# A decoder layer over 16 batches: approximate scores in four row groups, two bfloat16 transposes as DMAs

## What is computed

```python
# part 1: per head of 16 features: unit-length Fourier transforms of two projections,
#         one summed along the tokens, multiplied, transformed back, projected
q  = (x @ W_q.T).reshape(B, S, H, hd);  kv = (x @ W_kv.T).reshape(B, S, H, hd)
qf  = _l2_normalize_complex(fft(q));    kvf = cumsum(_l2_normalize_complex(fft(kv)), axis=1)
x = _layernorm(x + ifft(qf * kvf).real.reshape(B, S, D) @ W_o.T)
# part 2: causal attention of x on ctx, 16 heads of 16 features, keys = values = ctx
scores = jnp.einsum('bhqd,bhkd->bhqk', qh, kh) / math.sqrt(hd)
attn = softmax(where(causal, scores, MASKED_BIAS))
x = _layernorm(x + einsum('bhqk,bhkd->bhqd', attn, vh))
# part 3: x made ternary (threshold 0.33, +-0.5), times a ternary weight plus an offset
x_q = ternary_quantize(x, TH_X, SC_X)
x = _layernorm(x + jnp.einsum('bsd,od->bso', x_q, w_rram))
```

## Time and profile before

| | |
|---|---|
| median of 3 runs | 166.7 us (166.58 to 167.3) |
| the profiled execution | 166.76 us, its span 165.0 us |
| TensorE, VectorE, ScalarE, GpSimd busy | 146.9, 140.1, 128.2, 95.1 us |
| the chain that ended last | TensorE 47%, VectorE 28%, ScalarE 15%, issue 4%, GpSimd 4% |
| DMA | 14.56 MB, 29.5% of the 16 engines' span for the loads and stores |

### The profile page before, as it was taken

One profiled execution on the slowest core, in us unless ns is written; L12 is line 12 of the kernel. 1 busy time (PEld: TensorE's weight loads), 2 busy tenths in 40 slices (PEclk: granted clock), 3 DMA queues, 4 the chain that ended last, 5 costly groups with the idle time before them and its releaser, 6 DMA issues.

```text
span 165.0 us, 4546 instructions
## 1 busy us (share of the span) xinstructions
PE 146.9 (89%) x1612; PEld 98.6 (60%) x1629; DVE 140.1 (85%) x428; ACT 128.2 (78%) x342; POOL 95.1 (58%) x205
## 2 busy tenths in 40 slices
PE   7999999998999998999999999999899979897460
PEld 2746656567657556676776767765667647564230
DVE  0289899999999899989898989999899998868830
ACT  3466488888695986778989788878989979798642
POOL 4031550482690786156769834888477786778511
PEclk9999999999999999999999999999999999999855
DMA  3986566212033722122101554130312210101101
GB/s 107 288 270 177 175 161 216 79 52 68 0 116 106 204 63 60 35 57 76 36 0 38 162 156 99 56 105 2 90 41 43 96 28 2 36 32 36 64 34 64
DMA packets 16583, 14.56 MB, mean 88 GB/s; under 512 B 2352, under 2 KB 14512, under 8 KB 16560
## 3 DMA queue, kind: packets, MB, share of 16 engines
q1 hardware_dynamic: 16560, 14.26, 29.5%
HBM read 12.16 MB, written 2.10 MB: 86 GB/s over the span
## 4 chain that ended last, share of the span: by engine, by line
PE 47%; DVE 28%; ACT 15%; issue 4%; POOL 4%; POOLq 0%; ACTq 0%
PE p L727 8%; PE p L778 6%; PE p L747 6%; DVE x L2121 5%; ACT dev L1474 5%; PE p L762 5%; PE p L805 4%; PE p L768 3%; PE p L792 3%; ACT probs L1456 3%; PE p L785 3%; DVE ssq L2038 3%; PE p L733 2%; DVE unit L2054 2%; DVE r L2082 2%
## 5 line engine op out<-in xcount | busy, mean ns | idle before, releaser
L349 POOL TENSOR_SCALAR_AFFINE_SELECT probs<-probs 128x512 f32<-128x512 f32 x64 | 41.5, 664 | 10.1 <-ACT probs L1456 9.5
L2121 DVE TENSOR_REDUCE x<-p 128x4 f32<-128x512 f32 x64 | 41.7, 683 | 1.7 <-PE p L762 1.0
L1456 ACT ACTIVATE probs<-p 128x512 f32<-128x512 f32 x64 | 34.7, 595 | 4.7 <-PE p L778 4.5
L727 PE MATMUL p<-w_in,xT_s 128*128 128x512 f32 x64 | 30.3, 603 | 0.7 <-ACT w_in L1416 0.4
L343 POOL TENSOR_TENSOR rstd<-ve,power 128x1 f32<-128x1 f32 x48 | 26.9, 563 | 2.4
L338 POOL TENSOR_SCALAR ve<-spread 128x1 f32<-128x1 f32 x48 | 10.5, 218 | 29.6 <-ACT dev L1474 27.8
L1474 ACT ACTIVATE dev<-r,neg 128x256 f32<-128x256 f32 x48 | 24.2, 505 | 4.3 <-DVE neg L2094 4.2
L778 PE MATMUL p<-x1T,keys 32*128 32x128 f32 x512 | 18.8, 283 | 1.2 <-ACT x1T L1452 0.8
L778 PEld LDWEIGHTS p<-x1T,keys 32*128 32x128 f32 x512 | 15.8, 186 | 5.7 <-DVE x L2121 3.8
L785 PE MATMUL p<-probs,vals 128*32 128x128 f32 x512 | 18.1, 276 | 0.9 <-DVE att L2131 0.5
L762 PE MATMUL p<-keys,x1T_b 128*128 128x512 bf16 x47 | 16.4, 391 | 1.7 <-ACT probs L1456 1.1
(11 more groups left out here) (71 smaller groups left out, 282.8 us busy)
## 6 DMA issues: line engine op xcount, KB each, us to landing
vals<-ctxV SPq DMA_DIRECT2D x16, 256.0 KB, 2.9
x_s<-x SPq DMA_DIRECT2D x16, 128.0 KB, 2.7
xT_s<-xT SPq DMA_DIRECT2D x16, 128.0 KB, 2.6
keys<-ctxK SPq DMA_DIRECT2D x64, 32.0 KB, 2.2
out<-res SPq DMA_DIRECT2D x16, 128.0 KB, 1.7
wq_s<-w_q SPq DMA_DIRECT2D x1, 256.0 KB, 2.7
wkv_s<-w_kv SPq DMA_DIRECT2D x1, 256.0 KB, 3.7
woT_s<-w_oT SPq DMA_DIRECT2D x1, 256.0 KB, 3.9
```

Of the source, the lines that this page charges most:

```text
L349: nc.gpsimd.affine_select(out=part, in_=part, compare_op=ALU.is_ge, fill=0.0, base=0, pattern=[[0, GH], [1, TOK]], channel_multiplier=-1). ...
L727: last = nc.tensor.matmul(p[PROJ[n]][:], xT_s[n % XR][:, g, :], w_in[:, g, :], start=(g == 0), stop=(g == 1))
L1456: nc.scalar.activation(probs[n % 2][:, c, :, :].rearrange("p g q -> p (g q)"), p[ROWS + c][:], ACT.Exp, scale=HD ** -0.5).then_inc(exps[c], 1)
L2121: nc.vector.tensor_reduce(x1[n % X1R][:, GH * c:GH * (c + 1), HD], p[ROWS + c][:].rearrange("p (h k) -> p h k", h=GH), AX.X, ALU.max, nega ...
```

## The change

Five things change.

1. **Approximate scores.** `approximate(n)` is now one call with sixteen products: each takes one head's 32 rows and 128 columns, as `score` does. The head at slot s goes to the bank `APPROX[n][s]`. The key tile is compact, [128, 4, 128] instead of [128, 16, 128], and is loaded whole, constants included, with one DMA (256 KB instead of four times 32 KB). `blank`, `barred_s` and their waits are gone; the constants now encode nine queries to a slot. `row_max(n, c)` waits for one count after all sixteen.
2. **Banks.** The approximate and exact scores and the weighted values have banks by batch from all eight (`APPROX`, `SCORES`, `OUT`).
3. **Transposes.** `transpose_x1_b` and `transpose_xq` are DMAs from SBUF to SBUF in SP's queue, into `x1T_b` and `xqT_s`. TensorE's transposes and ScalarE's copies of both are gone.
4. **Start.** The folded input weights are copied half by VectorE, half by ScalarE. The first transposed inputs and the weights are loaded in another order. Rings of keys and values have six tiles, not five.
5. **Order.** All five lists are written in a new order.

```diff
-KV = 5
+KV = 6
...
+OUT = (0, 6, 0, 0, 5, 1, 1, 5, 2, 0, 2, 7, 1, 4, 2, 3)
+APPROX = ((0, 1, 7, 5), (2, 1, 4, 7), (6, 3, 5, 0), (1, 4, 3, 2), (5, 2, 0, 3), (1, 5, 6, 0),
...
-                for s in range(GH):
-                    sp.dma_start(keys[n % KV][SLOT * s:SLOT * s + HD, s::GH, :], ctxK[n, s]).then_inc(keys_in[n % KV], 16)
+                sp.dma_start(keys[n % KV][:], ctxK[n]).then_inc(keys_in[n % KV], 16)
...
+            def transpose_x1_b(n):
+                sp.dma_start_transpose(x1T_b[n % 2][:], x1_b[n % 2][:].rearrange("p h s -> p (h s)")).then_inc(x1T_b_in[n % 2], 16)
+
+            def transpose_xq(n):
+                sp.dma_start_transpose(xqT_s[n % 2][:], xq[n % 2][:]).then_inc(xqT_in[n % 2], 16)
...
-            def transpose_x1_b(n):
-
+            def approximate(n):
+
+                high = keys[n % KV][:].rearrange("p g k -> p (g k)").bitcast(bf16)[:, 1::2]
                 for g in range(GROUPS):
-                    last = nc.tensor.transpose(tile16(X1BT[n], GROUPS, TOK)[:, g, :],
-                                               x1_b[n % 2][:, GH * g:GH * (g + 1), :].rearrange("p h s -> p (h s)"),
-                                               ident_b[:])
-                last.then_inc(x1T_b_done, 1)
-
-            def approximate(n, c):
-
-                high = keys[n % KV][:, GH * c:GH * (c + 1), :].rearrange("p h k -> p (h k)").bitcast(bf16)
-                nc.tensor.matmul(p[ROWS + c][:], x1T_b[n % 2][:, c, :], high[:, 1::2],
-                                 start=True, stop=True).then_inc(approx[c], 1)
+                    for s in range(GH):
+                        slot = slice(SLOT * s, SLOT * (s + 1))
+                        last = nc.tensor.matmul(p[APPROX[n][s]][:, g * TOK:(g + 1) * TOK], x1T_b[n % 2][slot, g, :],
+                                                high[slot, g * TOK:(g + 1) * TOK], start=True, stop=True)
...
-            def transpose_xq(n):
-
-                for g in range(2):
-                    last = nc.tensor.transpose(tile16(XQT[n], 2, TOK)[:, g, :], xq[n % 2][:, g * 128:(g + 1) * 128], ident_b[:])
-                last.then_inc(xqT, 1)
 
...
-                        last = nc.tensor.matmul(p[ROWS + s][:, g * TOK:(g + 1) * TOK], keys[n % KV][slot, GH * g + s, :],
+                        last = nc.tensor.matmul(p[SCORES[n][s]][:, g * TOK:(g + 1) * TOK], keys[n % KV][slot, g, :],
...
-            def copy_x1T_b(n):
-
-                nc.scalar.activation(x1T_b[n % 2][:], tile16(X1BT[n], GROUPS, TOK), ACT.Copy).then_inc(x1T_b_copied, 1)
-
...
-            def copy_xqT(n):
-
-                nc.scalar.activation(xqT_s[n % 2][:], tile16(XQT[n], 2, TOK), ACT.Copy).then_inc(xqT_copied, 1)
...
-            def blank(buf):
-
-                nc.vector.tensor_copy(keys[buf][:], barred_s[:].unsqueeze(1).to_broadcast([128, HEADS, TOK])
-                                      ).then_inc(keys_blank[buf], 1)
+            def copy_w_in(g):
+
+                nc.vector.tensor_copy(w_in[:, g, :], p[g][:]).then_inc(w_in_ready[g], 1)
 
...
             def row_max(n, c):
 
-                nc.vector.tensor_reduce(x1[n % X1R][:, GH * c:GH * (c + 1), HD],
-                                        p[ROWS + c][:].rearrange("p (h k) -> p h k", h=GH), AX.X, ALU.max,
+                nc.vector.tensor_reduce(x1[n % X1R][:, c::GH, HD],
+                                        p[APPROX[n][c]][:].rearrange("p (h k) -> p h k", h=GH), AX.X, ALU.max,
                                         negate=True).then_inc(maxed[c], 1)
 
...
-    pairs = np.zeros((TOK, GH * SPARE), np.float32)
-    pairs[q, q // 3] = np.array([STEP_UP, 1.0, 1.0 / STEP_UP])[q % 3]
-    i, k = 3 * np.arange(GH * SPARE)[:, None], np.arange(TOK)[None, :]
-    bars = np.where(k > i + 2, -BARRED * STEP_UP,
-                    np.where(k == i + 2, -BARRED, np.where(k == i + 1, -LEAK, 0.0)))
-    barred = np.zeros((GH, SLOT, TOK), np.float32)
-    barred[:, HD, :] = 1.0
-    barred[:, HD + 1:, :] = bars.reshape(GH, SPARE, TOK)
-    trios = np.zeros((TOK, GH, SLOT - HD), np.float32)
-    trios[:, :, 1:] = pairs.reshape(TOK, GH, SPARE)
-    return trios, barred.reshape(GH * SLOT, TOK)
+    assert SHARE * SPARE >= TOK
+    pairs = np.zeros((TOK, SLOT - HD), np.float32)
+    pairs[q, 1 + q // SHARE] = 2.0 ** (TOP - STEP * (q % SHARE))
+    past = q[None, :] - SHARE * np.arange(SPARE)[:, None]
+    bars = np.where(past > 0, -2.0 ** (LEAK - TOP + STEP * np.clip(past, 0, SHARE)), 0.0)
+    return pairs, bars.astype(np.float32)
```

More of the change, by code:

```diff
@@ L149, in decoder_layer @@
         shift_done = [sem(f"shift_done{i}") for i in range(3)]
-        approx = [sem(f"approx{i}") for i in range(4)]
         maxed = [sem(f"maxed{i}") for i in range(4)]
@@ L215, in _ @@
-            sp.wait_ge(proj, 3)
-            load_xT(8)
+            load_x(4)
+            sp.wait_ge(x1_b_done, 1)
+            transpose_x1_b(0)
+            load_vals(1)
+            load_x(5)
+            load_x(6)
+            sp.wait_ge(x1_b_done, 2)
+            transpose_x1_b(1)
+            sp.wait_ge(x1_b_done, 3)
+            transpose_x1_b(2)
+            load_x(7)
+            load_keys(3)
+            load_x(8)
+            load_x(9)
+            load_keys(4)
+            load_keys(5)
@@ L809, in _ @@
             pe.wait_ge(warm_ready, 1)
-            busy(ROWS, 7)
+            busy(4, 7)
             pe.wait_ge(in_fold, 32)
@@ L976, in _ @@
+            pe.wait_ge(x1T_b_in[1], 48)
+            pe.wait_ge(keys_in[5], 16)
+            approximate(5)
+            pe.wait_ge(y_done, 9)
+            pe.wait_ge(x1T_copied, 4)
+            transpose_y(8)
+            pe.wait_ge(maxed[3], 5)
+            transpose_x1(4)
+            attend(7)
+            pe.wait_ge(maxed[3], 6)
             pe.wait_ge(masked[0], 3)
@@ new lines, in _ @@
+            cumulate(12)
+            pe.wait_ge(exps[2], 6)
+            pe.wait_ge(y_done, 12)
+            transpose_y(11)
+            pe.wait_ge(exps[3], 6)
+            pe.wait_ge(added[0], 11)
+            pe.wait_ge(x1T_b_in[1], 64)
+            pe.wait_ge(keys_in[1], 32)
+            approximate(7)
+            pe.wait_ge(added[2], 2)
+            transpose_x1(6)
+            pe.wait_ge(yT_copied, 12)
+            pe.wait_ge(xT_in[2], 48)
+            project(14)
+            pe.wait_ge(crossed, 13)
@@ new lines, in _ @@
+            pe.wait_ge(xT_in[3], 48)
+            project(15)
+            pe.wait_ge(maxed[0], 8)
+            pe.wait_ge(x1T_b_in[0], 80)
+            pe.wait_ge(keys_in[2], 32)
+            approximate(8)
+            pe.wait_ge(x1T_copied, 7)
+            pe.wait_ge(xqT_in[0], 32)
+            feed_forward(2)
+            pe.wait_ge(normed, 14)
+            attend(11)
+            pe.wait_ge(maxed[1], 9)
+            pe.wait_ge(y_done, 13)
+            transpose_y(12)
+            pe.wait_ge(added[2], 3)
@@ L1132, in _ @@
+            approximate(9)
+            pe.wait_ge(normed, 16)
+            pe.wait_ge(yT_copied, 14)
+            score(7)
+            pe.wait_ge(maxed[0], 10)
+            pe.wait_ge(masked[0], 7)
+            pe.wait_ge(vals_in[0], 32)
             weigh(6, 0)
+            weigh(6, 2)
+            pe.wait_ge(masked[3], 7)
             weigh(6, 3)
@@ L1274, in _ @@
+            pe.wait_ge(exps[1], 12)
+            pe.wait_ge(x1T_b_in[1], 112)
+            pe.wait_ge(keys_in[1], 48)
+            approximate(13)
+            pe.wait_ge(exps[2], 12)
+            pe.wait_ge(xqT_in[0], 64)
+            feed_forward(6)
+            weigh(10, 1)
+            weigh(10, 3)
+            pe.wait_ge(masked[2], 11)
+            weigh(10, 2)
+            pe.wait_ge(xqT_in[1], 64)
+            pe.wait_ge(exps[3], 12)
             feed_forward(7)
+            pe.wait_ge(maxed[3], 14)
@@ L2884 @@
     vals[..., HD] = 1.0
+    slots = np.zeros((BATCH, GH, SLOT, GROUPS, TOK), np.float32)
+    slots[:, :, :HD] = ctx.reshape(BATCH, TOK, GROUPS, GH, HD).transpose(0, 3, 4, 2, 1)
+    slots[:, :, HD] = 1.0
+    slots[:, :, HD + 1:] = bars[:, None, :]
     arrays = {
```

3044 lines of the change are left out of this document (1434 added, 1610 removed).

## The result

The changed kernel took 163.7 us (median of 4 executions, 162.0 to 164.9) against 166.7 before; the ratio is 0.973, 95% interval 0.968 to 0.979. The forecast was 162.1, with 156.5 to 169.0 around it. Six more executions of the same kernel in a later set gave 165.7 (163.9 to 166.3) beside 167.1, 0.990 [0.985, 0.994]; the median of all ten is 164.75. So the change is faster, by 1 to 2.7%, and the kernel with transposed DMAs scatters over 2.7% from execution to execution where the kernel before stays within 0.8% in every set. Since the ratios leave out what lies over 1.5% above a kernel's fastest, which here is ordinary scatter, I go by medians of all executions and give them beside the ratios.

What follows compares the result with a forecast made beforehand. VectorE and TensorE were taken to share the bound in the middle. Start 9.6, middle 128.0 and last stretch 22.7 gave a span of 160.3 us, time 162.1 with the 1.76 around it; range 156.5 to 169.

Steps and rivals of the forecast that it cites:

- Start: Time to VectorE's first sum of squares: 9.6 us instead of 10.13, with the two weight copies side by side.
- Middle: From VectorE's first sum of squares to its last row maximum: 121.0 us of VectorE work plus 7.0 idle, 128.0.
- that rival: TensorE, less busy, may be granted half clock speed in stretches: 168 us, chance 0.03.
- Last stretch: After VectorE's last row maximum: 21.3 us plus 1.4 for the last xq's uncovered landing, 22.7.
- The products: TensorE's sixteen approximate products of a batch: 0.55 us taken, at 35 ns each like the float32 exact scores.
- The landing: Transposed DMA in SP's queue, issue to landing: 2.9 us, as for 256 KB loads; outer ends 1.7 and twice 2.9.
- The rival of slow transposes: TensorE waits in order for transposed tiles, VectorE for its product; at 5.5 us a transpose, 172.7 us; chance 0.17.
- the two that I had called short: xq of batches 10 and 11: cover for the transposed landing about 0.8 us short each.
- my narrow ones: x1 of batches 0, 1 and 5: about 4 us of VectorE work as cover against 4.0 needed.
- my sign for wrong: SP's issue of a transpose over 1 us; another was TensorE waiting microseconds for DMA into x1T_b or xqT_s.
- Grouping: Rival: one count and four banks free at once delay row maxima 0.3 us a batch; 167.1 us, chance 0.13.
- it was not the bound: ScalarE falls from 128 to about 108 us without its copies; not the bound, it gives only earlier releases.

## Why the prediction was right, and which of its steps were not

The time was right in sign and within 1.6 us of the first set (2.7 of all ten), and part of that is luck: two errors of opposite sign. The profiled span, 163.2 us, is 2.9 above the forecast one: + 0.5 at the start, - 2.0 in the middle, + 4.4 at the end. The terms:

**Start, 9.6 forecast, 10.08 measured.** The two copies ran side by side only in part: VectorE's from 6.28, ScalarE's from 6.72, since the product it copies was ready only at 6.69. They ended at 7.32 instead of 7.37.

**Middle, 128.0 forecast, 126.0 measured.** The work was to be 121.0 and was 117.9; idle was to be 7.0 and was 8.1. The 12 instructions that moved behind the last row maximum account for 3.9 us (15.87 - 11.93) where I had 3.3. Most of the rest is overlap. Adding up the durations of the instructions that count as busy gives 166.5 us before and 163.9 after, while the busy time fell from 140.1 to 134.7: 26.4 us lay under a neighbour before, 29.2 after (2.1 of the 2.8 in the middle). My sum had no room for that. Why they overlap more was not tested; the order is the only thing that changed for most of them. Of the idle, 5.0 us came behind transposed tiles: 2.6 for approximate products and 2.4 for one feed-forward; what TensorE owed otherwise (y, r and rden, 2.0 us in the earlier trace rows) fell to 1.3. The last row maximum ended at 136.1 against 137.6, but VectorE was 93.5% busy up to it, not over 95%, and TensorE's busy time was 134.6 us, not 125 to 130. That sign did not follow from my own terms: 146.9 - 12.8 is 134.1. The clock was full up to there; that rival did not come in the middle.

**Last stretch, 22.7 forecast, 27.1 measured.** This is the step that failed, the mis-sized term. I took 3.3 us of work out of the middle and added none at the end, as if the end had been empty. Even with xq on TensorE the stretch is 23.65 us, 2.35 more than before's 21.3. With both transposes on TensorE it is 25.20, 3.9 more, while the middle is 129.33, 4.2 less: nearly all that left the middle there came back at the end. And I counted one uncovered landing (1.4 us). The order makes it two, one behind the other, and undoing xq's DMAs took 3.45 us off. VectorE's list, just ahead of the piece of it that I read, has the addition of 13 in front of xq 14; I read what stood between xq 15 and its own addition.

The clock has a part in the 3.45. In the first profile it was granted at half from 148.7 us on, before at half from 155.2, with xq on TensorE from 153.6; in the 3 us before it fell TensorE was busy for 1.31, 1.37 and 1.23 us. A feed-forward takes 1.46 us at half and 0.83 at full clock; three ran at half in the changed kernel, one with xq on TensorE, which is 1.3 us. In the second profile two did, and its last stretch was 26.69 us: 3.04 more than with xq on TensorE, 0.6 of it the clock's. So at least 2.2 to 2.4 us are the landings'.

**The products.** From start to start 0.34 us for sixteen, against 0.55 taken:

```profile
69.03 0.41 PE L827 MATMUL p<-keys,x1T_b 32*128 32x128 bf16 x16
69.37 0.70 PE L803 MATMUL p<-unit,upto_s 128*128 128x256 f32 x2
```

The 35 ns of the float32 passes was too dear; the Trainium skill's 3.07x (TensorE: Matmul & The Clock Gate), by which I had 0.30, was nearer. As forecast, the sum did not hang on it: 5.4 us more cost 0 to 2.

**The landing.** 2.9 us taken, medians 3.0 and 2.8 measured. The rule of the Trainium skill (VectorE: DVE Perf Modes, The three transpose paths) of 1309 ns a block, 5.2 us for four by my estimate, does not hold for these: four blocks land in 2.4 us and two in 2.3 when nothing is in the way, so blocks do not follow one another. The rival of slow transposes is wrong as stated, but its mechanism, TensorE waiting in order, came with single landings of 4 to 6 us and with the end. TensorE's 12.5 us of waits for xq are 6.1 for batches 13 to 15, 2.4 and 2.2 for 1 and 5, which I had called covered, and 0.9 each for 7 and 10; of the two that I had called short, 11 showed none. For x1 they are 0.8, 1.3 and 1.7 us in batches 1, 4 and 10, of which only 1 was among my narrow ones.

**SP's issue.** I took that it issues like a copy, 0.43 us; it is 1.17 to 1.19 us. This was my sign for wrong, and it showed. So did the other, TensorE waiting for xqT_s for microseconds. The issues made no bound by themselves (32 of them are 38 us of the queue), but 9% of the chain is SP's.

**Grouping.** The products' wait for four free banks stayed small: VectorE waited 2.6 us in all for the approximate products, 1.5 us of it for x1 10, which landed 4.6 us after its issue, not for banks.

**What the DMAs bring.** I credited ScalarE's relief with earlier releases and no time. It is worth 1.8 to 4 us (0.024 of 167). The step that failed there is "it was not the bound": sixteen copies more, 10.0 us, that nobody waits for cost time on an engine that was 73% busy and became 77%. ScalarE itself fell to 112.1 us, not to 108.

So the total came out near because errors cancelled in part: the middle's overlap on one side, the end on the other. The mechanism was half right: TensorE did get slack, but without the DMAs the rest of the change gave 0.8 us, and with them 1.4 to 3.0.

## What to carry to other kernels

Here transposed DMAs paid where mostly several microseconds of other work lay between source and reader, and took load off two engines there (undoing the three of x1 without cover changed nothing); in the last batches, where every step is a latency, the detour over TensorE and ScalarE is shorter. Decide it per tensor, and for the last batches by themselves: here x1 by DMA and xq on TensorE gave 160 to 161 us against 165 for both by DMA and 166 for both on TensorE. When instructions move out of a full stretch, add them to the stretch they move to, and read what stands ahead of the last batches' sources, not only behind them. Before crediting waits, try both ways: x1's DMA showed 3.7 us of waits and saved 5 to 7.
